# Causal attention heads: bias skewed through SBUF lines, band compacted in memory, fewer stores

## The reference, cut to what matters

```python
scores = jnp.einsum('bhqd,bhkd->bhqk', q, k)
rel_idx = jnp.clip(pos[None, :] - pos[:, None], -MAX_REL_POS, MAX_REL_POS) + MAX_REL_POS
rel = rel_emb[rel_idx]
scores = scores + jnp.einsum('bhqd,qkd->bhqk', q, rel)
causal = jnp.tril(jnp.ones((L, L), dtype=bool))
scores = jnp.where(causal[None, None], scores, NEG_INF)
attn = jax.nn.softmax(scores, axis=-1)
ctx = jnp.einsum('bhqk,bhkd->bhqd', attn, v)
ctx = ctx + jnp.einsum('bhqk,qkd->bhqd', attn, rel)
out = ctx.transpose(0, 2, 1, 3).reshape(B, L, MODEL_DIM) @ w_o.T
```

## Time and profile before

| | us |
|---|---|
| median of 3 runs | 5097.98 (5095.38 to 5112.85) |
| profiled execution, own time | 5106.48 |
| its span | 5104.8 |
| moe 0, moe 1 | 529, 522 |
| causal heads: to the end of head 0 | 147 |
| causal heads: heads 1 to 27 | 1298 (48.1 each) |
| causal heads: heads 28 to 31 and end | 151 |
| causal projection | 143 |

### The profile page before, as it was taken

How to read it: one execution, slowest core, us unless ns; L and a number is a source line. 1 busy time by engine, 2 the same in 40 slices (tenths; PEclk the granted TensorE clock), 3 DMA queues, 4 the chain that set the end, 5 groups by cost and what they waited for, 6 DMA issues and landing times. The chain is left out here.

```text
span 5104.8 us, 80050 instructions
## 1 busy us (share of the span) xinstructions
PE 4455.2 (87%) x25680; PEld 2625.2 (51%) x25680; DVE 2996.9 (59%) x5384; ACT 2297.0 (45%) x4375; POOL 648.1 (13%) x666
## 2 busy tenths in 40 slices
PE   7999859999999999889998965688978978889488
PEld 6888723333333333258886544345545545555355
DVE  6655668888888888456664355444444544444342
ACT  3222327777777777612222222334434434445222
POOL 2322100000000000013332024111111111111000
PEclk9999969999999999889999987778778878789699
DMA  2000311111111111039000026444444444341801
GB/s 77 0 0 1 138 50 42 42 39 41 37 37 42 42 38 33 11 113 296 0 0 18 0 86 183 112 93 93 103 95 95 105 94 96 97 98 44 133 26 33
DMA packets 316682, 343.08 MB, mean 67 GB/s; under 512 B 161280, under 2 KB 266760, under 8 KB 302600
## 3 DMA queue, kind: packets, MB, share of 16 engines
q1 hardware_dynamic: 299912, 296.20, 22.1%
q0 software_dynamic: 16384, 41.96, 2.9%
HBM read 239.26 MB, written 148.11 MB: 76 GB/s over the span
## 5 line engine op out<-in xcount | busy, mean ns | idle before, releaser
L1322 DVE TENSOR_REDUCE full_tops<-psum 128x1 f32<-128x1024 f32 x1024 | 1207.2, 1220 | 247.8 <-PE psum L1226 247.4
L1279 ACT ACTIVATE full_probs<-psum 128x512 f32<-128x512 f32 x2048 | 1067.2, 602 | 338.5 <-PE psum L1198 306.4
L1736 ACT ACTIVATE causal_probs<-psum 128x512 f32<-128x512 f32 (+3 forms) x1280 | 644.3, 533 | 761.2 <-PE psum L1622 389.4
L1784 DVE TENSOR_REDUCE causal_tops<-psum 128x1 f32<-128x1024 f32 (+7 forms) x704 | 587.4, 859 | 261.5 <-PE psum L1659 261.5
L1198 PE MATMUL psum<-full_q,full_k 49*128 49x512 f32 x2048 | 657.8, 482 | 49.5 <-ACT full_probs L1279 33.3
L1608 PE MATMUL psum<-causal_q,causal_k 49*128 49x512 f32 (+3 forms) x1280 | 465.3, 508 | 181.2 <-DMA causal_q<-causal_rows 171.0
L1198 PEld LDWEIGHTS psum<-full_q,full_k 49*128 49x128 f32 x2048 | 290.1, 189 | 640.4 <-ACT full_probs L1279 585.4
L1207 PE MATMUL psum<-full_probs,full_vh 128*32 128x512 f32 x4096 | 565.3, 625 | 0.7 <-ACT full_probs L1279 0.7
L1226 PE MATMUL psum<-full_k,full_q 48*128 48x512 f32 x2048 | 408.9, 463 | 64.7 <-DMA full_k<-qk_split 38.3
L1659 PE MATMUL psum<-causal_k,causal_q 48*128 48x512 f32 (+4 forms) x1152 | 375.2, 468 | 88.9 <-DMA causal_k<-rot_parts 46.9
L1638 PE MATMUL psum<-causal_probs,causal_vh 128*32 128x384 f32 (+3 forms) x3712 | 409.1, 501 | 1.2 <-ACT causal_probs L1736 1.2
(11 more groups left out here) (189 smaller groups left out, 6095.6 us busy)
## 6 DMA issues: line engine op xcount, KB each, us to landing
bias_tiles<-in_bias SPq DMA_DIRECT2D x4, 10240.0 KB, 86.5
causal_bias<-bias_tiles SPq DMA_DIRECT2D x32, 1280.0 KB, 27.7
band_scores<-xn POOLq DMA_DIRECT2D x192, 160.0 KB, 6.1
qk_split<-qkvf_parts SPq DMA_DIRECT2D x32, 512.0 KB, 3.4
full_q<-qk_split SPq DMA_DIRECT2D x64, 256.0 KB
full_k<-qk_split SPq DMA_DIRECT2D x64, 256.0 KB
rot_parts<-qkvc_parts SPq DMA_DIRECT2D x32, 512.0 KB, 3.1
causal_q<-rot_parts SPq DMA_DIRECT2D x64, 256.0 KB
```

The source lines that it names most:

```text
L1279: nc.scalar.activation(pT[:, kt % 4, n * BLK:(n + 1) * BLK], k.psum[:, bank(q, u), :], ACT.Exp).then_inc(p_ready, 1)
L1322: nc.vector.reduce_max(mx[:, q % 2, u // 2, u % 2:u % 2 + 1], src, AX_X).then_inc(m_free, 1)
L1736: nc.scalar.activation(dst, k.psum[:, bank(q, u), 0:(hi - lo) * P], ACT.Exp).then_inc(p_ready, 1)
L1784: last = nc.vector.reduce_max(mx[:, r, t, entry:entry + 1], both[:, off:off + hi - lo], AX_X)
```

## The change

- The fill of `bias_tiles` in moe 1 is gone. The mask now lies in SBUF (80 KB), and a line of 8 tiles of mask per partition in `skew_rows`, [128, 1281].
- Per head, `load_rel` loads the relative scores (256 KB) into `compact` in SBUF. DVE's `spread(i, part)` copies half of them (128 x 8 x 32) into the gaps of `skew_rows`. `skew(i, part)` writes the lines to `bias_tiles`, 128 lines of 1280 or 1281 elements, where a row of the buffer is 16 x 160 + 1 elements: the line is one element longer than it is read, which makes the skew. The bias is read as 128 lines of 2560 elements (`load_bias`).
- There is one `skew_rows` buffer: `spread(i, 1)` waits until the line transfer `skew(i, 0)` has landed (`skewed`), and SP's `skew(i, part)` waits for `spread_done`. In DVE's list of body i the two spreads of head i+4 stand behind the third unit and behind the ninth.
- SP's order in a body: `load(i+3)`, `load_bias(i+3)`, `skew(i+4, 0)`, `store(i-1)` (4 transfers of 17 rows, numerators and denominator together, into `causal_heads`), `skew(i+4, 1)`, `load_rel(i+5)`, `row_load(i+1)`.
- Band tiles have 4 pairs of buffers instead of 8; the output has one buffer instead of two. POOL issues per head one more transfer, `compact_band`: `band_scores` to `band_compact`, 2048 pieces of 128 B, memory to memory. The causal projection reads it in 1 transfer per block instead of 4, in pieces of 512 B.
- ACT copies the row one step's pair of exponentials earlier. The full attention's projection loads its reciprocals repeated, without the matmul; DVE reads them from SBUF.

```diff
-                if run == 1:
-                    fill_bias_tiles(k, sp)
...
+                def load_rel(i):
+                    if not isinstance(i, int) or i > 0:
+                        sp.wait_ge(spread_done, 2 * i)
+                    sp.dma_start(compact[:, :, :], k.TD[bass.ds(i, 1), :, :, :].rearrange("a p t j -> p (a t) j")).then_inc(rel_loaded, 16)
+
+                def skew(i, part):
+                    sp.wait_ge(spread_done, 2 * i + part + 1)
+                    lines = k.BB[1:1 + NH * P * BIAS_ROW].rearrange("(h p x) -> h p x", h=NH, p=P)
+                    dst = lines[bass.ds(i, 1), :, part * HALF_ROW:(part + 1) * HALF_ROW + part].rearrange("a p x -> (a p) x")
+                    sp.dma_start(dst, skew_rows[:, 0:HALF_ROW + part]).then_inc(skewed, 16)
+
+                def load_bias(i, q):
+                    heads = k.BB[0:NH * P * BIAS_ROW].rearrange("(h x) -> h x", h=NH)
+                    src = heads[bass.ds(i, 1), 0:P * KT * BAND].rearrange("a (r t c) -> (a r) t c", r=P, c=BAND)
+                    sp.dma_start(bt[:, q, :, :], src).then_inc(bt_loaded[q], 16)
...
-                        sp.dma_start(cols(k.ND[bass.ds(j * DH, DH), :]), blocks(osb[32 * b:32 * b + DH, r, :])).then_inc(o_stored[r], 16)
-                        sp.dma_start(cols(k.DD[bass.ds(j, 1), :]), blocks(osb[32 * b + DH:32 * b + VW, r, :])).then_inc(o_stored[r], 16)
+                        dst = k.OD[bass.ds(j, 1), :, :].rearrange("a r (m b n) -> (a r) m b n", b=QB, n=P)[:, :, b, :]
+                        src = osb[32 * b:32 * b + VW, :].rearrange("r (m n) -> r m n", n=P)
+                        sp.dma_start(dst, src).then_inc(o_stored, 16)
...
-                def body(i, q):
-                    load(i + 3, (q + 3) % 4)
-                    store(i - 1, (q + 1) % 2)
-                    row_load(i + 1, (q + 1) % 4)
+                def body(i, q, left):
+                    if left > 2:
+                        sp.wait_ge(skewed, 32 * (i + 4))
+                        sp.wait_ge(pv_done, (i + 3) * NSTEP + NSTEP)
+                        load(i + 3, (q + 3) % 4)
+                        load_bias(i + 3, (q + 3) % 4)
+                    if left > 3:
+                        skew(i + 4, 0)
+                    store(i - 1)
+                    if left > 3:
+                        skew(i + 4, 1)
+                    if left > 4:
+                        load_rel(i + 5)
+                    if left:
+                        row_load(i + 1, (q + 1) % 4)
...
+                def compact_band(i, q):
+                    for n in range(PAIRS, NSTEP):
+                        pool.wait_ge(band_stored[n], 16 * (i + 1))
...
+                    src = k.PB[bass.ds(i * KT, KT), 1:1 + P * SKEW].rearrange("t (r c) -> r t c", c=SKEW)[:, :, 0:REL]
+                    dst = k.CD[bass.ds(i, 1), :, :, :].rearrange("a p t j -> p (a t) j")
+                    pool.dma_start(dst, src).then_inc(k.compacted[q], 16)
...
+                def spread(i, part):
+                    if part == 0:
+                        dve.wait_ge(rel_loaded, 16 * (i + 1))
+                    if not isinstance(i, int) or i + part > 0:
+                        dve.wait_ge(skewed, 16 * (2 * i + part))
+                    nc.vector.memset(skew_rows[:, HALF_ROW:HALF_ROW + 1], 0.0)
+                    wide = skew_rows[:, 0:HALF_ROW].rearrange("p (t c) -> p t c", c=BAND)
+                    tiles = slice(part * KT // 2, (part + 1) * KT // 2)
+                    nc.vector.tensor_copy(wide[:, :, 0:REL], compact[:, tiles, :]).then_inc(spread_done, 1)
...
                 def body(i, q, left):
-                    for ahead, h, p in segment(q, left):
+                    more = not isinstance(i, int) or i + 4 < NH
+                    for at, (ahead, h, p) in enumerate(segment(q, left)):
                         if p == 1 and ahead == 2:
                             tops(i + 1, (q + 1) % 4)
                         far(i + ahead, h, p)
+                        if at in (2, 8) and more:
+                            spread(i + 4, at // 8)
...
-                    for t in range(TB):
-                        tile = bass.DynSlice(batch(n) * H * KT + within(n) * TB + t, H, KT)
-                        src = k.PB[tile, 1:1 + P * SKEW].rearrange("h (r c) -> r h c", c=SKEW)[:, :, 0:REL]
-                        sp.dma_start(wt[:, half, t, :].rearrange("p (h j) -> p h j", h=H), src).then_inc(s_wt[half], 16)
+                    src = k.CD[bass.ds(batch(n) * H, H), :, bass.ds(within(n) * TB, TB), :].rearrange("h p t j -> p h (t j)")
+                    sp.dma_start(wt[:, half, :, :, :].rearrange("p h t j -> p h (t j)"), src).then_inc(s_wt[half], 16)
```

More of the change, by code:

```diff
@@ L1447, in heads_causal_stage @@
         o_free = sem("o_free")
-        o_stored = [sem(f"o_stored{r}") for r in range(2)]
+        o_stored = sem("o_stored")
         mm_stored = [sem(f"mm_stored{r}") for r in range(2)]
@@ L1464, in band_tile @@
         def band_tile(n, i):
-            o = 2 * n + i
-            return head[:, o, :] if o < KT - 4 else tail[:, o - (KT - 4), :]
+            return bands[:, 2 * (n % PAIRS) + i, :]
         def band_pair(n):
-            o = 2 * n
-            return head[:, o:o + 2, :] if o < KT - 4 else tail[:, o - (KT - 4):o - (KT - 4) + 2, :]
+            return bands[:, 2 * (n % PAIRS):2 * (n % PAIRS) + 2, :]
         def segment(q, left):
@@ L1529, in _ @@
                 sp.wait_ge(ones, 4)
-                for q in range(3):
-                    load(q, q)
+                load(0, 0)
+                skew(0, 0)
+                skew(0, 1)
+                load_rel(1)
+                load(1, 1)
+                sp.wait_ge(skewed, 32)
+                sp.wait_ge(edge_set, 16)
+                load_bias(0, 0)
+                skew(1, 0)
+                skew(1, 1)
+                load_rel(2)
+                load(2, 2)
+                sp.wait_ge(skewed, 64)
@@ L1532, in _ @@
+                load_bias(1, 1)
+                skew(2, 0)
+                skew(2, 1)
+                load_rel(3)
+                sp.wait_ge(skewed, 96)
+                load_bias(2, 2)
                 row_load(0, 0)
                 load(3, 3)
-                row_load(1, 1)
-                def body(i, q):
-                    load(i + 3, (q + 3) % 4)
-                    store(i - 1, (q + 1) % 2)
-                    row_load(i + 1, (q + 1) % 4)
+                skew(3, 0)
+                skew(3, 1)
@@ new lines, in _ @@
+                load_rel(4)
+                sp.wait_ge(skewed, 128)
+                load_bias(3, 3)
+                skew(4, 0)
+                skew(4, 1)
+                load_rel(5)
+                row_load(1, 1)
+                def body(i, q, left):
[13 more added lines that the diff above has]
+                        row_load(i + 1, (q + 1) % 4)
@@ L1552, in _ @@
-                store(NH - 1, (NH - 1) % 2)
+                        body(it * 4 + q, q % 4, 5)
+                for i in range(NH - 7, NH):
+                    body(i, i % 4, NH - 1 - i)
+                store(NH - 1)
+                sp.wait_ge(o_stored, 16 * QB * (NH + 1))
                 for r in range(2):
-                    sp.wait_ge(o_stored[r], 16 * (1 + 2 * QB * NH // 2))
                     sp.wait_ge(mm_stored[r], 16 * (1 + NH // 2))
@@ L1788, in far @@
                             dve.wait_ge(bt_loaded[q], 16 * (i // 4 + 1))
-                        if not first:
-                            dve.wait_ge(band_stored[n], 16 * i)
-                        nc.vector.memset(turn[:, r, n:n + 1], 0.0)
+                        if n >= PAIRS:
+                            dve.wait_ge(band_stored[n - PAIRS], 16 * (i + 1))
+                        elif not first:
+                            dve.wait_ge(band_stored[n + PAIRS], 16 * i)
+                        if n == 0:
+                            nc.vector.memset(band_tile(0, 0)[:, 0:REL], NEG)
+                        else:
+                            nc.vector.memset(turn[:, r, n:n + 1], 0.0)
                         for side, t in enumerate(pieces):
@@ L1896, in load @@
                 src = k.RD[bass.ds(batch(n) * H, H), cols]
-                sp.dma_start(rd[0:HC, half, :, :], src.rearrange("(c h) n -> h c n", h=HC)).then_inc(s_ld[half], 16)
+                for c in range(C):
+                    every = src[c * HC:(c + 1) * HC, :].unsqueeze(1).to_broadcast([HC, DH, BLK])
+                    sp.dma_start(rd[:, half, c, :], every).then_inc(s_ld[half], 16)
             with sp.Fori(0, NBLK // 2) as it:
@@ L1908, in blockwise @@
             def blockwise(n, half, last):
-                pe.wait_ge(s_ld[half], 32 * (n // 2 + 1))
-                for c in range(C):
-                    pe.wait_ge(o_ready, 2 * C + (n - 1) * C + c + 1)
-                    nc.tensor.matmul(k.psum[:, c, :], spread[0:HC, :], rd[0:HC, half, c, :],
-                                     start=True, stop=True).then_inc(rb_ready, 1)
```

(2 more changed lines are left out.)

128 lines of the change are left out of this document (62 added, 66 removed).

## The result

| | before | after |
|---|---|---|
| median of 4 runs each (us) | 5097.97 | 5405.24 |
| lowest to highest | 5095.38 to 5112.85 | 5386.67 to 5437.96 |
| profiled execution, its span | 5104.8 | 5392.8 |
| head 0 ends at | 3285.8 | 3311.8 |
| heads 1 to 27, per head | 48.1 | 57.6 |

The changed kernel is slower: ratio 1.0603, 95% interval 1.0544 to 1.0662. A head is counted from the end of the head before it, where ScalarE begins the copy of that head's output. Between the profiled spans lie 288.0 us: heads 1 to 27 hold 257.7 of them, the time up to the end of head 0 25.9, the last heads 0.3, the projection 0.8, and the second LSTM and the final store 3.3.

A forecast was written before the change was run, and what follows sets the result against it. No engine was full; PE waited for the row because SP was held behind q/k draining on two engines. 5106.5 + 402 + 50 - 20 - 8 = 5530.5, 8.5 above the median of runs, so 5522 us; range 5250 to 5720.

The forecast's parts named there:

- head term: Heads 1 to 27: 63 us each instead of 48.1, +402 us; outermost bounds +124 and +770, middling +213 and +591.
- What bounds the kernel before: Causal heads: no engine full; PE waits 146 us for the row, as SP is held behind q/k on two engines.
- The prize of 13.5 us a head: Causal heads: with SP free, a head would take 34.6 us instead of 48.1.
- The new wait: DVE's second spread waits for the line transfer behind q/k, landing at 34 us: DVE stands 21 us in each head.
- The rest of a head and the clock: Each causal head after the landing: 21 us of remaining work plus 8 us for lower clock (0 to 19).
- SP's list: SP's own work falls from 41 to about 15 us per head; waits for the row go; no cost.
- The rival of a hold at the bias: SP stays held, line transfer issued at 28 us, landing by 36.3: 65.3 us a head, 5584 us; chance 0.13.
- Start of the stage: Before and in head 0, bias and line transfers wait behind q/k loads: +50 us, from 25 to 75.
- Last four heads: Heads 28 to 31, which have no spread: 0, plus or minus 12 us.
- Causal projection: Shorter band transfer saves 2.5 us in each of 8 blocks: -20 us (0 to -35); blocks take 10 to 11 us.
- Full projection and fill: Full attention's projection without its spreading matmuls: -8 us; removing the fill in moe 1: 0.
- Faster: Rival: line transfer lands before DVE asks, at 15 to 16 us; heads 35.5 us, 4730 us in all; chance 0.11.

The follow-up runs named there:

- experiment 5: Kernel before, with only the q/k tensor's memory layout changed to go by heads: 4856.78 us, ratio 0.9504.
- Experiment 1: Changed kernel, with the first line transfer of a head issued ahead of the q/k loads and bias: 5299.97 us, ratio 1.0408.
- experiment 12: Kernel before, with only the compact band and the causal projection's one transfer per block added: 5097.02 us, ratio 1.0013.
- experiment 9: Changed kernel, q/k laid out by heads, compute engines' loop of 8 heads instead of 4, q/k and bias issued last: 4740.83 us, ratio 0.9306.
- experiment 2: Changed kernel, with first line transfer and the four output stores issued ahead of q/k and bias: 5311.0 us, ratio 1.0428.
- experiment 4: Changed kernel, order untouched, with the q/k tensor's memory layout by heads: 4989.64 us, ratio 0.9808.
- Experiment 10: Kernel before, q/k laid out by heads, loop of 8 heads, q/k, bias and skew issued behind stores and row: 4830.9 us, ratio 0.9485.

## Why the prediction was right, and where it was not

The side and the mechanism were right, the size was 117 us too large (5522 against 5405.24), within the range of 5250 to 5720. That range took its lower end from the outermost bound of the head term (+124) and its upper from a middling one (+591); with the middling lower end (+213) it would begin near 5330 and still hold the measurement.

- **What bounds the kernel before.** Right in the main: experiment 5 shows that q/k on two engines made two thirds of the hold. The prize of 13.5 us a head was too high for the mean: 7.6 came (48.1 to 40.5), though 14 of 27 heads reach 35.0 to 36.6.
- **The new wait.** Right in place and cause: part 0 takes 24.4 us in the median, part 1 6.5, PE stopped 15.3 us into the head (3327.1) for a forecast of 15. That the total, 556.5 us, meets the forecast of about 550 is luck (the list names no releaser for these waits, where the forecast had the transfer's name): 68.9 of it are three waits before head 1, and in heads 1 to 27 there are 487.6, 18 a head for a forecast of 21. The landing was mis-sized: 31.7 us after the start against 34. I had 31.7 as the lower end, from q/k's drain and two engines' shares, and took the middle towards the old skew's 36.6, but the lines didn't need the extra time that I added for the 2048 pieces. That the lower end came true to a tenth is luck, for its 27 us of drain was 26.2 in the earlier trace rows, rounded up and read in another stage. 27 x 2.3 = 62 us.
- **The rest of a head and the clock.** 21 + 8 = 29 us forecast, 25.9 measured (57.6 less 31.7). Head 1, from 3311.8, had 21.3, just the warm rest; head 19 had 35.3, with the same work at half clock (1.2 GHz):

```profile
3343.10:3364.40 21.30, 20.42 (x164) 12.29 (x166) 14.32 (x42) 10.92 (x22) 3.63 (x5) 0.89 0.27 90
4374.70:4410.00 35.30, 33.10 (x162) 18.51 (x162) 14.33 (x42) 11.09 (x23) 3.63 (x5) 0.50 0.17 55
```

So, if the warm rest is 21, the clock's term was about 5 in the mean, where I took 8: 27 x 3.1 = 84 us for rest and clock together. The granted clock, 0.74, was within the forecast of 0.7 to 0.8.
- **SP's list.** Half wrong, without cost. I gave the hold a small chance and priced SP at 15 us of its own work; it was held 25 us, in the stores, until 33.0 us and not 27. As the text said for that case, the row was needed later (it was ready at 40.1 and issued 0.3 us later). The rival of a hold at the bias that delays the line transfer didn't come: part 0 was issued 7.1 us into the head. Experiment 1 shows what the hold costs when nothing covers it.
- **Start of the stage.** +50 forecast, about +28 measured (25.9 at the end of head 0, and 2 us had been won before the stage). PE stopped twice before its first score, 26.9 and 23.7 us, and once more in head 0, 15.0 us, for bands that waited on line transfers, but that first score came only 13.4 us later than before, at 3254.8.
- **Last four heads.** 0 forecast, +0.3.
- **Causal projection.** -20 forecast, +0.8 measured. Two steps failed: the transfer of 7 us was 5.4 or 10.8 to 12.3, and a block isn't shorter by what its transfer is: VectorE doesn't wait for the band at all in every second block, and yet the turns from the third block on are 11.7 to 15.5 us, not 10 to 11. What bounds such a block instead was not isolated.
- **Full projection and fill.** -8 and 0 forecast, together -2.
- **The sum.** Head term 402 forecast, 257.7 measured; start 22 less; projections 27 more; LSTM 3 more: 424 - 144 - 22 + 27 + 3 = 288.
- **The rivals.** Faster fell, for its condition (landing by 19 us) was missed by 12.7. Experiment 1 shows that the condition can be had (part 0 lands in 3.0 to 4.4 us, by 12 us of a head), and that even then the time doesn't come, because the row of maxima takes the wait over; that rival's 4730 had no such step in it. The minimum of 512 B a piece, which the Trainium skill's page "DMA: Bandwidth & Descriptors" gives in "Specifications", decided nothing here: lines of 5 KB behind q/k waited 24 us, and the projection's pieces of 512 B for 128 B brought nothing (experiment 12). No rival gave the change a better order; with it, the new layout and the longer loop, experiment 9 beats both kernels.

## What to carry to other kernels

Ahead of shortening a transfer that holds a queue, read what it stands behind: if DMA is almost idle while everybody waits (share 0.13), look for a transfer whose memory side begins with a dimension of 2, and lay that tensor out anew; here that was worth 5% on the kernel before and 7.5% on the changed one (0.9808 / 1.0603). With the layout as it was, the three orders tried chose who pays, and the best of them only drew level with the kernel before. And where one bound is worked out from the mechanism and the other is a neighbour's row, ask what the neighbour has that the new transfer lacks before taking the middle.

## What the runs showed of the hardware

Whether an issue is held depends on what is issued, and not only on what is queued ahead. Four stores of 34 KB held the sync engine 25 us behind q/k and took 5 us ahead of them (experiment 2), while a line transfer of 640 KB was issued in 0.36 us behind the same q/k and bias, in the changed kernel and in experiment 2. What sets the stores and the old skew apart was not tested. To land is another matter: behind q/k a row of 8 KB waited 23 us, as long as 640 KB did.

PE's idle time at a loop's jump differs with the place of the loads: 1.3 to 2.9 us with q/k issued at the head's start in experiment 5 (up to 4.2 in experiment 4), but 6.0 and 6.2 us in experiment 9, where they are issued in the last third of the head before:

```profile
3520.89 1.10 PE L1660 MATMUL psum<-causal_q,causal_k 49*128 49x512 f32 x3 [6.01 <-issue]
3804.42 1.11 PE L1660 MATMUL psum<-causal_q,causal_k 49*128 49x512 f32 x3 [6.21 <-issue]
```

Experiment 10, with the same place of the loads, has 6.1 and 6.6. Just ahead of the first of these gaps the DMA share is 0.98, and during it 0.66, with packets of 8 and 16 KB on the queues that the page lists as "instruction"; the last of them ends 0.3 us before PE goes on. That the gap is PE's own instructions being loaded behind the other transfers fits this, but no run tested it.
